# Second up-product bank, down products two units behind, and a copy moved behind the exponentials, in a four-layer attention and convolution kernel

## The chip, the cores and the metric

The kernel runs on one core of one Trainium2 chip, in one launch. The metric is the device time of that core in microseconds (us). Below, PE is TensorE, PEld its weight load, DVE VectorE, ACT ScalarE, POOL GpSimd, SP SyncE.

## The reference, cut to what matters

The input is 16 images of 128 channels by 32x32 points (1024 tokens each), float32. Four layers run one after the other; the change touches the first and the last.

```python
x = conv_attention(x)            # layer 0: group norm, qkv, softmax attention with 8 heads, projection, residual
x = x + large_kernel_conv(gn(x)) # layer 1: depthwise convolutions, gate, 1x1
t = t + landmark_attention(ln(t)); t = t + gelu_experts(ln(t))   # layer 2, 8 experts, 2 of them per token
t = t + plain_attention(ln(t))   # layer 3: q = x W + b, keys and values are the tokens themselves
t = t + silu_experts(ln(t))      # layer 3: 16 experts of width 64, 6 per token, and 2 shared ones
```

In the last line each expert computes `down(silu(gate(x)) * up(x))`, weighted by its routing score.

## The kernel before

**First stage** (`attention_phase`, about 0 to 2160 us). For each image two groups of four heads run in 64 slots. In each slot PE makes one tile of unshifted scores for a later group (L627), whose row maxima DVE takes (L454), and one tile of shifted scores (L683); ACT takes the exponentials of the two 512-column halves of that tile (L589); every fourth slot PE weighs values with them (L696). Other work of the next and the previous image is hung on single slots by `plan`. For the next image, ACT evicts the q product in slot 4 and the k product in slot 6: L565 writes `full`, L567 then copies it as bfloat16 into `pieces[:, qk, 0, :]`, and the semaphore `full_up` lets POOL cut the remaining two pieces (`split`, L399 and L401). After the second split POOL divides the previous image's sums (`divide`, L388). Both L565 and L567 stand ahead of the two exponentials of their slot on ACT.

**Last stage** (`dense_attention_and_silu`, from about 4413 us to the end; the change's title calls it the third stage). The experts are computed densely. Two experts form one unit of width 128; 8 units and one unit of shared experts make 9 (`UNITS`), and the two 512-token halves make 18 steps per image (`STEPS`). A step has three slots:

- slot 0: PE makes the gate product into the bank `ps_g` (L2214), and ACT takes its silu into one of two `act_up` buffers (L2094);
- slot 1: PE makes the up product into the single bank `ps_u` (L2217), and DVE multiplies it into `act_up` (L2021, or L2024 for the shared unit) and raises `u_read`;
- slot 2: DVE multiplies by the scores into one of two `mixed` buffers (L2028, `mixed_up`), and PE makes the down product of the step before (L2201, `down(i, n - 1)`), accumulated over 9 steps in `ps_o`.

The up product of step n waits until DVE has read the bank in step n - 1. The silu of step n waits for `mixed` of step n - 2.

Beside the steps of image i run coroutines, resumed by slot number (`due`): `choice(i + 1)`, the router (on DVE four passes over 2048 elements, L1012, L1013, L1017, L1019, and a reduction L1021), and `attention(i + 2)`: its layer norm on DVE in the first slots (L961, L966, L973), its first transposes from slot 9, its eight 128-row tiles from slot 15 on (PE L2146, L2152, L2159; DVE L1963, L1966, L1973; ACT L2056, L2059), and a second layer norm on DVE from slot 40 on. After slot 53 PE makes the last down product, DVE copies the next image's tile (`hand_over`, L2010) and the next image begins. Image 14 has only `choice` beside it, image 15 nothing. All engines run their own program in order.

The function that starts the last stage gives it PSUM banks, and buffers that earlier layers no longer use. The bank `ps_xy` was used by the layer before (L1791, L1608) and is idle in the last stage.

Of the kernel before, what the change touches and what calls it, by code (L numbers as in the profile page):

```python
# [97 lines left out]
def attention_phase(nc, sems, handles, B, io, const, const_in, band_dram, u_cols, gn2, x1_dram, split_dram, sums_dram, conv):  # L98
# [3 lines left out]
    with ExitStack() as st:  # L102
# [445 lines left out]
        def _(act):  # L548
# [9 lines left out]

            def step(work, i, nxt, prev, n, parity):
                if work[0] == "qk":  # L560
# [6 lines left out]
                    act.activation(pieces[:, qk, 0, :], full[:, qk, :], ACT.Copy)  # L567
                    act.drain().then_inc(full_up, 1)
# [14 lines left out]
            def body(kind, i):  # L583
                front, n = kind != "last", 0
                for m, works in enumerate(bodies[kind]):
                    n = run(works, kind, i, n)
                    for k in range(HALVES):
                        act.wait_ge(b_up, i * (2 * SLOTS) + 2 * m + k + 1)
                        act.activation(probs[:, m % PROBS, 512 * k:512 * k + 512], ps_b[:, k, :], ACT.Exp).then_inc(b_exp, 1)  # L589
                    if kind == "first" and m >= QUAD and m % 2 == 0 and (m - QUAD) // 2 < BANDS:  # L590
                        store_rows((m - QUAD) // 2)
# [448 lines left out]
def landmark_and_gelu_phase(nc, ctx, B, io, const, maps, gn2, x1_dram, x_dram, y_dram, score_dram, out):  # L1040
# [7 lines left out]
    with ExitStack() as st:  # L1048
# [3 lines left out]
        def sem(name):  # L1052
# [99 lines left out]
            nc, ctx, st, B, io, const, tokens, score_dram, out, flat(0, 17), (stats, mv, var, inv, tmp), (pa, pb_, *ps_h, pc), score_t, ones,  # L1152
            dict(xln=xln, xt=xt, qt=qt, probs=probs, probs_t=probs_t, xln2=tiled(kt[:, :]), xt2=wide(v[:, :, :]),
                 wg=tok_next, wu=tok, wd=tiled(xt2[:, :]), scores=up_weights, xt_now=part(0), tile_in=tiled(part(1)),
                 act_up=part(2).rearrange("p (a n) -> p a n", a=2), mixed=part(3).rearrange("p (a n) -> p a n", a=2),
# [478 lines left out]
        def _(pe):  # L1634
# [190 lines left out]
            down(B - 1, LAST)  # L1825
            run_dense()


def dense_attention_and_silu(nc, ctx, st, B, io, const, tokens, score_dram, out, small, norm, banks, score_t, ones, shared):
# [18 lines left out]
    RING = 4  # L1848
# [101 lines left out]
    def vector(dve):  # L1950
# [61 lines left out]
        def experts(i, stages):  # L2012
            for slot in range(SLOTS):
                n = slot // 3
                k, unit = divmod(n, UNITS)
                if slot % 3 == 1:
# [3 lines left out]
                    if unit < PAIRS:  # L2020
                        dve.tensor_tensor(act_up[:, n % 2, :], act_up[:, n % 2, :], ps_u[:, :], ALU.mult).then_inc(u_read, 1)  # L2021
                        dve.drain()  # L2022
                    else:
                        dve.scalar_tensor_tensor(mixed[:, n % 2, :], act_up[:, n % 2, :], 0.5, ps_u[:, :], ALU.mult, ALU.mult).then_inc(u_read, 1)  # L2024
                        dve.drain().then_inc(mixed_up, 1)
                if slot % 3 == 2 and unit < PAIRS:
                    dve.wait_ge(scores_in[unit % RING], i * (16 * HALVES * PAIRS * 2 // RING) + 32 * (k * (PAIRS // RING) + unit // RING) + 32)
                    dve.tensor_tensor(mixed[:, n % 2, :], act_up[:, n % 2, :], scores[:, unit % RING, :], ALU.mult).then_inc(mixed_up, 1)  # L2028
# [7 lines left out]
        def run(sums):  # L2036
            dve.sem_inc(u_read, 1)
# [4 lines left out]
    def scalar(act):  # L2042
# [43 lines left out]
        def experts(i, stages):  # L2086
            for slot in range(SLOTS):
                n = slot // 3
                if slot % 3 == 0:
# [5 lines left out]
                    if n == UNITS + 1:  # L2095
# [17 lines left out]
    def tensor(pe):  # L2113
# [75 lines left out]
        def down(i, n):  # L2189
# [11 lines left out]
            last = pe.matmul(ps_o[:, :], wd(unit), mixed[:, n % 2, :], start=False, stop=(unit == UNITS - 1), skip_group_check=True)  # L2201
# [3 lines left out]
        def experts(i, stages):  # L2205
            pe.wait_ge(S["xt_handed"], i + 1)
            for slot in range(SLOTS):
# [7 lines left out]
                if part == 1:  # L2215
                    pe.wait_ge(u_read, i * STEPS + n + 1)
                    pe.matmul(ps_u[:, :], wu(unit), xt_now[:, cols], start=True, stop=True).then_inc(u_ps, 1)  # L2217
                if part == 2:
                    if n:
                        down(i, n - 1)  # L2220
                for stage in stages:
                    due(stage, slot)
# [91 lines left out]
```

## Time and profile before

| | |
|---|---|
| median of 3 runs | 6012.23 us (6007.84 to 6017.8) |
| the profiled execution's own time | 6006.96 us |
| its span, first to last instruction | 6005.2 us |
| mean granted TensorE clock | 0.914 of full |
| busy: PE, DVE, ACT, POOL | 83%, 60%, 50%, 17% of the span |

A line of a group view gives: source line, engine, operation, output and inputs, count, busy time, mean duration, and the idle time of the engine just ahead of it with what ended it. In a timeline, the first number is the start, the second the duration (from first start to last end where instructions are merged, as "x8" says), and the bracket is the idle time before. A float32 matmul is shown as two passes (x2), whose modelled duration overlaps the next one's start: in the steady state one 512-column product starts 0.86 us after the one before, though its row says 1.02 us. Names of tensors are those of the memory: `n_ps_h` stands for both `ps_g` and `ps_u`, `n_ps_c` for `ps_o`, `n_down_weights` for `act_up`, `mixed` and others, `n_up_weights` for the scores.

### The profile page before, as it was taken

The numbers are of one execution on the slowest core, as the hardware profiler recorded it, in microseconds if no ns is written. First come the engines' busy times: TensorE is split into PE (matmuls) and PEld (weight loads), VectorE is DVE, ScalarE is ACT, GpSimd is POOL, SyncE is SP. The second block draws the span as 40 slices with busy tenths as digits, with TensorE's granted clock in tenths as the row PEclk, the third lists the DMA queues.
The fourth block names the chain that finished last, engine by engine and source line by source line (L and its number), as shares of the span: only waits on it lengthen the run. The fifth ranks groups of instructions, "written<-read, shape, count | busy, mean of one in ns | idle before, by whom it ended". The sixth has DMA issues, their size and how long they took to land.

```text
span 6005.2 us, 81857 instructions
## 1 busy us (share of the span) xinstructions
PE 4989.7 (83%) x25633; PEld 2720.5 (45%) x25633; DVE 3604.7 (60%) x7715; ACT 3005.7 (50%) x5436; POOL 1011.5 (17%) x1348
## 2 busy tenths in 40 slices
PE   5888888888888869577777777777888999999899
PEld 1222222222222223376676666766665555545454
DVE  6677667777767725544454444444456667676665
ACT  2555555555655534144444444444564555545453
POOL 2111122111122022022322323223210000000000
PEclk7999999999999989688888888888899999999999
DMA  2422222222222112234344334433321111111112
GB/s 78 139 80 65 75 70 91 65 86 65 65 76 85 48 38 28 62 114 131 113 121 129 116 113 132 118 114 113 100 59 48 43 49 48 44 48 45 48 45 71
DMA packets 406297, 477.10 MB, mean 79 GB/s; under 512 B 87640, under 2 KB 249648, under 8 KB 403760
## 3 DMA queue, kind: packets, MB, share of 16 engines
q1 hardware_dynamic: 372128, 424.84, 23.4%
q0 software_dynamic: 20576, 35.55, 2.1%
q10 hardware_dynamic: 13168, 11.48, 0.7%
q8 instruction: 214, 3.51, 0.2%
q14 instruction: 211, 1.73, 0.1%
HBM read 308.54 MB, written 145.57 MB: 76 GB/s over the span
## 4 chain that ended last, share of the span: by engine, by line
PE 34%; DVE 11%; another core or an unknown queue 6%; issue 4%; DVEq 2%; ACT 2%; ACTq 0%; SPq 0%; DMA 0%
PE n_ps_xy L1791 4%; PE n_ps_h L1781 4%; PE n_ps_f L2159 3%; PE n_ps_f L2152 3%; PE n_ps_c L2201 3%; PE n_ps_h L2217 3%; PE n_ps_h L2214 3%; PE n_ps_f L2146 2%; PE n_ps_f L1639 2%; PE n_ps_f L985 1%; DVE n_down_weights L2021 1%; DVE n_stats L961 1%; ACT n_hidden L1594 1%; DVEq L2022 1%
## 5 line engine op out<-in xcount | busy, mean ns | idle before, releaser
L589 ACT ACTIVATE a_probs<-ps_b 128x512 f32<-128x512 f32 x2048 | 1110.9, 594 | 805.5 <-PE ps_b L683 793.1
L454 DVE TENSOR_REDUCE a_negmax<-ps_a 128x1 f32<-128x1024 f32 x1024 | 1207.3, 1220 | 400.2 <-PE ps_a L627 390.6
L627 PE MATMUL ps_a<-a_k_stack,a_q_stack 96*128 96x512 bf16 x2048 | 640.0, 399 | 176.3 <-DVE a_negmax L454 82.9
L683 PE MATMUL ps_b<-a_q_stack,a_k_stack 99*128 99x512 bf16 x2048 | 679.8, 392 | 85.3 <-ACT a_probs L589 42.8
L1594 ACT ACTIVATE n_hidden<-n_ps_h,n_b 128x128 f32<-128x128 f32 x1472 | 420.0, 374 | 409.0 <-PE n_ps_h L1781 314.3
L696 PE MATMUL ps_o<-a_probs,a_v_ones 128*32 128x512 f32 x4096 | 561.8, 622 | 0.2 <-ACT a_probs L589 0.2
L1791 PE MATMUL n_ps_xy<-n_down_weights,n_hidden 128*128 x2944 | 436.8, 295 | 94.7 <-ACT n_xy L1608 53.9
L627 PEld LDWEIGHTS ps_a<-a_k_stack,a_q_stack 96*128 96x128 bf16 x2048 | 148.5, 99 | 732.1 <-DVE a_negmax L454 453.7
L1781 PE MATMUL n_ps_h<-n_xy,n_up_weights 128*128 128x128 f32 x2944 | 436.1, 293 | 36.6 <-issue 36.1
L1791 PEld LDWEIGHTS n_ps_xy<-n_down_weights,n_hidden 128*128 128x128 f32 x2944 | 394.9, 207 | 133.7 <-issue 130.6
L683 PEld LDWEIGHTS ps_b<-a_q_stack,a_k_stack 99*128 99x128 bf16 x2048 | 196.8, 100 | 510.1 <-ACT a_probs L589 281.3
L1781 PEld LDWEIGHTS n_ps_h<-n_xy,n_up_weights 128*128 128x128 f32 x2944 | 395.3, 206 | 60.2 <-issue 57.6
L2094 ACT ACTIVATE n_down_weights<-n_ps_h 128x512 f32<-128x512 f32 x288 | 172.4, 598 | 491.6 <-PE n_ps_h L2214 489.2
L1299 POOL DMA_INDIRECT rows_scratch<-n_xln,n_index_out x256 | 253.2, 989 | 843.8 <-DVE n_index_out L1452 766.9
L1291 POOL DMA_INDIRECT n_rows<-outs_scratch,n_index_back x256 | 255.7, 999 | 680.4 <-DMA outs_scratch<-n_xy 536.4
L2201 PE MATMUL n_ps_c<-n_down_weights,n_xt 128*128 128x512 f32 x512 | 285.1, 640 | 67.7 <-DVE n_down_weights L2028 67.6
L2217 PE MATMUL n_ps_h<-n_down_weights,n_tok 128*128 128x512 f32 x512 | 278.2, 626 | 61.8 <-DVE n_down_weights L2021 61.8
L410 POOL CAST a_shift<-a_shift 16x128 bf16<-16x128 f32 x192 | 54.2, 283 | 1335.2 <-DVEq L463 1317.8
L2159 PEld LDWEIGHTS n_ps_f<-n_xln,n_u_probs_t 128*128 128x128 f32 x2048 | 248.0, 193 | 59.9 <-issue 44.4
L2214 PE MATMUL n_ps_h<-n_down_weights,n_tok_next 128*128 128x512 f32 x512 | 273.3, 617 | 1.5 <-ACT n_down_weights L2079 1.5
L2159 PE MATMUL n_ps_f<-n_xln,n_u_probs_t 128*128 128x128 f32 x2048 | 253.0, 277 | 1.6 <-ACT n_u_probs_t L2056 1.6
L2152 PE MATMUL n_ps_f<-n_qt 128*128 128x512 f32 x512 | 242.4, 596 | 0.0
(324 smaller groups left out, 7342.3 us busy)
## 6 DMA issues: line engine op xcount, KB each, us to landing
n_up_weights<-in_L_ffn_W_dram SPq DMA_DIRECT2D x368, 256.0 KB
n_up_weights<-score_scratch SPq DMA_DIRECT2D x512, 128.0 KB
split_scratch<-a_pieces SPq DMA_DIRECT2D x180, 256.0 KB
a_q_stack<-split_scratch SPq DMA_DIRECT2D x128, 192.0 KB, 3.3
a_k_stack<-split_scratch SPq DMA_DIRECT2D x128, 192.0 KB, 3.9
rows_scratch<-n_zero SPq DMA_DIRECT2D x16, 1472.0 KB, 8.2
outs_scratch<-n_xy SPq DMA_DIRECT2D x176, 128.0 KB
n_xg<-rows_scratch SPq DMA_DIRECT2D x80, 256.0 KB
```

Of the source, the lines that this page charges most:

```text
L454: dve.tensor_reduce(negmax[:, b, t:t + 1], bank, axis=AX.X, op=ALU.max, negate=True).then_inc(ring_read, 1)
L589: act.activation(probs[:, m % PROBS, 512 * k:512 * k + 512], ps_b[:, k, :], ACT.Exp).then_inc(b_exp, 1)
L627: last = pe.matmul(bank[:, cols], q_stack[0:KS, h, 128 * t:128 * t + 128], k_stack[0:KS, h, cols], start=True, stop=True)
L683: pe.matmul(ps_b[:, k, :], k_stack[:, h, 128 * t:128 * t + 128], q_stack[:, h, 512 * k:512 * k + 512], start=True, stop=True).then_inc(b_u ...
L696: last = pe.matmul(ps_o[32 * j:32 * j + 32, 512 * k:512 * k + 512], v_ones[:, t, J * g + j, :], probs[:, (J * quad + j) % PROBS, 512 * k:5 ...
L1594: last = act.activation(hidden[:, j % 2, f, :], ps_h[j % 2][:, 128 * f:128 * f + 128], ACT.Gelu, bias=b1[:, bass.ds(e, 1), f:f + 1].rearra ...
L1781: last = pe.matmul(ps_h[j % 2][:, 128 * f:128 * f + 128], up_weights[:, j % RING, 128 * f:128 * f + 128], rows_t, start=True, stop=True)
L1791: last = pe.matmul(ps_xy[:, col:col + 128], hidden[:, j % 2, f, :], own_down[:, f, :], start=(f == 0), stop=(f == FT - 1))
L2159: last = pe.matmul(pb[:, 0:C], probs_t[:, (t - 1) % 2, m, :], xln[:, m, :], start=(m == 0), stop=(m == NT - 1))
L2201: last = pe.matmul(ps_o[:, :], wd(unit), mixed[:, n % 2, :], start=False, stop=(unit == UNITS - 1), skip_group_check=True)
L2214: pe.matmul(ps_g[:, :], wg(unit), xt_now[:, cols], start=True, stop=True).then_inc(g_ps, 1)
L2217: pe.matmul(ps_u[:, :], wu(unit), xt_now[:, cols], start=True, stop=True).then_inc(u_ps, 1)
```

## The change

In the last stage the up products alternate between two banks (`ps_h[1]` and `ps_xy`), so that the one of step n waits for DVE's reading of step n - 2. The down product of step n - 2, no longer n - 1, stands in slot 2 of step n, and two of them follow after the last slot. `mixed` has three buffers, the third in a tile of the layer before. The eviction of the first half's result on ACT moves one step later. PE waits before the stage until `ps_xy` has been emptied. In the first stage the copy L567 goes behind the two exponentials of its slot, except where the image's own prologue runs.

```diff
+            pending = []
+
+            def first_piece(qk):
+                act.activation(pieces[:, qk, 0, :], full[:, qk, :], ACT.Copy)
+                act.drain().then_inc(full_up, 1)
...
-                    act.activation(pieces[:, qk, 0, :], full[:, qk, :], ACT.Copy)
-                    act.drain().then_inc(full_up, 1)
+                    if i == nxt:
+                        first_piece(qk)
+                    else:
+                        pending.append(qk)
...
                         act.activation(probs[:, m % PROBS, 512 * k:512 * k + 512], ps_b[:, k, :], ACT.Exp).then_inc(b_exp, 1)
+                    if pending:
+                        first_piece(pending.pop())
...
-            nc, ctx, st, B, io, const, tokens, score_dram, out, flat(0, 17), (stats, mv, var, inv, tmp), (pa, pb_, *ps_h, pc), score_t, ones,
+            nc, ctx, st, B, io, const, tokens, score_dram, out, flat(0, 17), (stats, mv, var, inv, tmp), (pa, pb_, ps_h[0], (ps_h[1], ps_xy), pc), score_t, ones,
...
+            pe.wait_ge(moved, B * PAIRS + 2)
             run_dense()
...
-                        dve.tensor_tensor(act_up[:, n % 2, :], act_up[:, n % 2, :], ps_u[:, :], ALU.mult).then_inc(u_read, 1)
+                        dve.tensor_tensor(act_up[:, n % 2, :], act_up[:, n % 2, :], ps_u[n % 2][:, :], ALU.mult).then_inc(u_read, 1)
...
-                    dve.tensor_tensor(mixed[:, n % 2, :], act_up[:, n % 2, :], scores[:, unit % RING, :], ALU.mult).then_inc(mixed_up, 1)
+                    dve.tensor_tensor(mixed[(i * STEPS + n) % 3], act_up[:, n % 2, :], scores[:, unit % RING, :], ALU.mult).then_inc(mixed_up, 1)
...
-            dve.sem_inc(u_read, 1)
...
-                    if n == UNITS + 1:
+                    if n == UNITS + 2:
                         store_half(i, 0)
...
-                    pe.wait_ge(u_read, i * STEPS + n + 1)
-                    pe.matmul(ps_u[:, :], wu(unit), xt_now[:, cols], start=True, stop=True).then_inc(u_ps, 1)
+                    if started(i) or n >= 2:
+                        pe.wait_ge(u_read, i * STEPS + n - 1)
+                    pe.matmul(ps_u[n % 2][:, :], wu(unit), xt_now[:, cols], start=True, stop=True).then_inc(u_ps, 1)
                 if part == 2:
-                    if n:
-                        down(i, n - 1)
+                    if n >= 2:
+                        down(i, n - 2)
                 for stage in stages:
                     due(stage, slot)
+            down(i, STEPS - 2)
             down(i, STEPS - 1)
```

## Rows read from the trace of the kernel before

**Rows 1.** The page: span, and each engine's busy time.

```profile
span 6005.2 us, 81857 instructions
PE 4989.7 (83%) x25633; PEld 2720.5 (45%) x25633; DVE 3604.7 (60%) x7715; ACT 3005.7 (50%) x5436; POOL 1011.5 (17%) x1348
```

**Rows 2.** Window, images 0 to 14: length, busy PE, PEld, DVE, ACT, POOL, clock.

```profile
4413.00:5950.00 1537.00, 1390.48 (x5702) 791.04 (x5702) 1027.08 (x2383) 780.98 (x979) 15.22 (x16) 0.97 0.15 49
```

**Rows 3.** Waits of PE from 4413 us on: total us, times, longest.

```profile
PE n_ps_c L2201 <- DVE n_down_weights L2028: 67.6, 49, 3.9
PE n_ps_h L2217 <- DVE n_down_weights L2021: 61.8, 28, 12.0
```

**Rows 4.** Windows of one image of the last stage, in three stretches.

```profile
5143.50:5162.60 19.10, 15.10 (x33) 5.91 (x32) 12.30 (x46) 3.45 (x5) 0.00 (x0) 0.91 0.18 55
5162.60:5192.40 29.80, 25.70 (x85) 12.83 (x83) 25.83 (x58) 12.64 (x17) 0.00 (x0) 0.94 0.17 51
5192.40:5247.50 55.10, 54.38 (x277) 35.50 (x278) 31.92 (x61) 38.40 (x47) 0.00 (x0) 1.00 0.13 41
```

**Rows 5.** Timeline of the end of one image, PE and DVE, from step 13 on.

```profile
5144.70 1.65 DVE L961 BATCH_NORM_STATS2 n_stats<-maps 128x6 f32<-128x128 f32 x8
...
5151.08 0.69 DVE L2021 TENSOR_TENSOR n_down_weights<-n_down_weights,n_ps_h 128x512 f32<-128x512 f32 x1
...
5151.82 1.12 PE L2217 MATMUL n_ps_h<-n_down_weights,n_tok 128*128 128x512 f32 x2 [2.84 <-DVE n_down_weights L2021]
...
5155.13 1.92 PE L2214 MATMUL n_ps_h<-n_down_weights,n_tok_next 128*128 128x512 f32 x2
...
5158.28 0.69 DVE L2021 TENSOR_TENSOR n_down_weights<-n_down_weights,n_ps_h 128x512 f32<-128x512 f32 x1 [2.02 <-PE n_ps_h L2217]
...
5160.86 0.69 DVE L2024 SCALAR_TENSOR_TENSOR n_down_weights<-n_down_weights,n_ps_h 128x512 f32<-128x512 f32 x1 [1.10 <-PE n_ps_h L2217]
...
5162.61 1.02 PE L2214 MATMUL n_ps_h<-n_down_weights,n_tok_next 128*128 128x512 f32 x2
```

**Rows 6.** Timeline of the start of the next image, up to its first attention tiles.

```profile
5165.47 0.69 DVE L2021 TENSOR_TENSOR n_down_weights<-n_down_weights,n_ps_h 128x512 f32<-128x512 f32 x1 [0.42 <-PE n_ps_h L2217]
...
5175.66 0.69 DVE L2021 TENSOR_TENSOR n_down_weights<-n_down_weights,n_ps_h 128x512 f32<-128x512 f32 x1 [0.66 <-ACT n_down_weights L2094]
...
5186.26 0.69 DVE L2021 TENSOR_TENSOR n_down_weights<-n_down_weights,n_ps_h 128x512 f32<-128x512 f32 x1 [0.77 <-PE n_ps_h L2217]
...
5189.89 1.22 DVE L1966 TENSOR_REDUCE e_negmax<-n_ps_f 128x1 f32<-128x1024 f32 x1
...
5192.41 1.09 PE L2146 MATMUL n_ps_f<-c_ident,n_yt_probs 128*128 128x128 f32 x8 [0.25 <-ACT n_yt_probs L2059]
```

**Rows 7.** Waits of DVE from 4413 us on.

```profile
DVE n_down_weights L2021 <- PE n_ps_h L2217: 79.8, 83, 3.8
...
DVE n_down_weights L2024 <- PE n_ps_h L2217: 19.1, 18, 1.1
```

**Rows 8.** Waits of PE from 5895 to 5950 us: image 14, with only the router beside it.

```profile
PE n_ps_c L2201 <- DVE n_down_weights L2028: 5.9, 3, 3.9
```

**Rows 9.** Timeline of image 15: two gate products, one step apart.

```profile
5990.35 1.02 PE L2214 MATMUL n_ps_h<-n_down_weights,n_tok_next 128*128 128x512 f32 x2
...
5992.93 1.02 PE L2214 MATMUL n_ps_h<-n_down_weights,n_tok_next 128*128 128x512 f32 x2
```

**Rows 10.** Timeline of the first stage around one k product: ACT, PE, POOL.

```profile
1018.75 1.11 ACT L565 ACTIVATE a_full<-ps_a,a_kbias 128x1024 f32<-128x1024 f32 x1 [1.96 <-PE ps_a L653]
...
1019.95 1.06 ACT L567 ACTIVATE a_pieces<-a_full 128x1024 bf16<-128x1024 f32 x1
...
1021.11 3.31 ACT L589 ACTIVATE a_probs<-ps_b 128x512 f32<-128x512 f32 x6
...
1021.76 0.88 PE L683 MATMUL ps_b<-a_q_stack,a_k_stack 99*128 99x512 bf16 x2 [0.75 <-ACT a_probs L589]
...
1031.72 2.47 POOL L388 TENSOR_TENSOR a_o_sums<-a_o_sums,a_recips 128x256 f32<-128x256 f32 x3 [1.21 <-DMA a_recips<-sums_scratch]
```

More of the change, by code:

```diff
@@ L1151, in landmark_and_gelu_phase @@
         dense = dense_attention_and_silu(
-            nc, ctx, st, B, io, const, tokens, score_dram, out, flat(0, 17), (stats, mv, var, inv, tmp), (pa, pb_, *ps_h, pc), score_t, ones,
+            nc, ctx, st, B, io, const, tokens, score_dram, out, flat(0, 17), (stats, mv, var, inv, tmp), (pa, pb_, ps_h[0], (ps_h[1], ps_xy), pc), score_t, ones,
             dict(xln=xln, xt=xt, qt=qt, probs=probs, probs_t=probs_t, xln2=tiled(kt[:, :]), xt2=wide(v[:, :, :]),
                  wg=tok_next, wu=tok, wd=tiled(xt2[:, :]), scores=up_weights, xt_now=part(0), tile_in=tiled(part(1)),
-                 act_up=part(2).rearrange("p (a n) -> p a n", a=2), mixed=part(3).rearrange("p (a n) -> p a n", a=2),
+                 act_up=part(2).rearrange("p (a n) -> p a n", a=2), mixed=[part(3)[:, 0:512], part(3)[:, 512:1024], xg[:, 0, :, :].rearrange("p t c -> p (t c)")],
                  result=hidden[:, :, :, :].rearrange("p a f n -> p a (f n)")))
@@ L2020, in experts @@
                     if unit < PAIRS:
-                        dve.tensor_tensor(act_up[:, n % 2, :], act_up[:, n % 2, :], ps_u[:, :], ALU.mult).then_inc(u_read, 1)
+                        dve.tensor_tensor(act_up[:, n % 2, :], act_up[:, n % 2, :], ps_u[n % 2][:, :], ALU.mult).then_inc(u_read, 1)
                         dve.drain()
                     else:
-                        dve.scalar_tensor_tensor(mixed[:, n % 2, :], act_up[:, n % 2, :], 0.5, ps_u[:, :], ALU.mult, ALU.mult).then_inc(u_read, 1)
+                        dve.scalar_tensor_tensor(mixed[(i * STEPS + n) % 3], act_up[:, n % 2, :], 0.5, ps_u[n % 2][:, :], ALU.mult, ALU.mult).then_inc(u_read, 1)
                         dve.drain().then_inc(mixed_up, 1)
@@ L2200, in down @@
             pe.wait_ge(mixed_up, i * STEPS + n + 1)
-            last = pe.matmul(ps_o[:, :], wd(unit), mixed[:, n % 2, :], start=False, stop=(unit == UNITS - 1), skip_group_check=True)
+            last = pe.matmul(ps_o[:, :], wd(unit), mixed[(i * STEPS + n) % 3], start=False, stop=(unit == UNITS - 1), skip_group_check=True)
             if unit == UNITS - 1:
```

## The prediction

> **What bounds the kernel now.** I read the page first, then windows by stage, then the waits of the last stage, then one image of it in the timeline. The page has PE busy for 83% of the span and DVE for 60% [rows 1], but these are means over stages. In the last stage, images 0 to 14, PE is busy 1390 of 1537 us [rows 2], so about 147 us are idle there. Most of that idle time is two waits for DVE: 67.6 us before down products and 61.8 us before up products, 129.4 us together [rows 3]. These are the two waits that the change moves by a unit. The temptation is to subtract them. Whether they can be had depends on what DVE is doing meanwhile.
>
> One image shows it. Its period is 104.0 us (19.10 + 29.80 + 55.10) and falls into three stretches [rows 4]. In the third, the attention tiles, PE is busy 54.38 of 55.10 us at full clock: PE is the bound and nothing is to be had. In the second, the router, DVE is busy 25.83 of 29.80 us. In the first, the layer norm at the image's end, PE is busy 15.10 and DVE 12.30 of 19.10 us, the clock is at 0.91, and DVE waits for PE as well as PE for DVE. So outside the tiles the two engines share a chain. Once the up product has a second bank, PE waits less, but DVE's own work stays in line and becomes the bound. What the change can give back is then the time in which DVE itself stood waiting for an up product, and not the time in which PE stood waiting for DVE.
>
> **The change part by part.**
>
> *End of an image (steps 13 to 17).* DVE starts the layer norm at 5144.70 and reaches the multiplication of step 14 only at 5151.08; PE's up product of step 14 + 1 waits for exactly that and starts at 5151.82 after 2.84 us of idling [rows 5]. From there PE is a unit late: DVE waits 2.02 us for the up product of step 16 and 1.10 us for that of step 17 [rows 5]. In the new order the up product of step 16 needs only the reading of step 14, which is over at 5151.08 + 0.69 = 5151.77. It can start near 5151.8, and DVE wants it at 5158.28 - 2.02 = 5156.26: ready. The up product of step 17 needs the reading of step 15. The silu of each step still waits for the second multiplication of two steps before, which here precedes by more than the 0.60 us of a silu, so ACT does not take over. DVE's chain then runs without these waits and closes 2.02 + 1.10 = 3.12 us earlier. PE can follow: from 5144.70 to the next image's first gate product it has 14 products at 0.86 us (a third of the 2.58 us between the gate products of image 15 [rows 9]), 12.0 us, and 5144.7 + 12.0 = 5156.7 is ahead of 5162.61 - 3.12 = 5159.49. Both trailing down products fit: the second-last one runs while DVE does L2024, the last one follows it as today. What may be lost is clock. In this stretch the clock is granted at 0.91, so 0.09 x 19.10 = 1.7 us of PE work is missing [rows 4]; a gate product at the lower of its two levels (1.2 instead of 2.4 GHz) takes 1.92 instead of 1.02 us [rows 5]. PE still idles some 2.8 us there afterwards (5159.49 - 5156.7), so a half-clock stretch probably stays. PE has that slack only until the last products, which it can make late by part of the 1.7 us. Bounds 3.12 and 3.12 - 1.7 = 1.4 us; I take 2.7, since most of the slack lies ahead of the last three products.
>
> *Start of an image (steps 0 to 5).* DVE waits 0.42 us for the very first up product, which no second bank makes earlier, 0.66 us for a silu that stands on ACT behind the router's exponential and its table, and 0.77 us for the up product of step 4 [rows 6]. The first two stay. The third goes, as PE is a unit ahead by then. PE's other idle time there only changes place: it will run ahead, make the early products of the attention, and then stand before the transposes of tile 1, which wait for the exponential that follows DVE's maximum L1966 (5189.89) [rows 6]. That maximum is behind the router passes on DVE, and DVE is in line for it. So the start gives 0.77 us at best, 0 at worst if PE's half clock just there eats it; I take 0.75.
>
> *The tiles.* PE's order has one down product shifted by a unit and the same number of them. Nothing.
>
> Together 2.7 + 0.75 = 3.45 us per image, for images 0 to 13: 48.3 us. A check from the other side: over the stage DVE waits 79.8 + 19.1 = 98.9 us for up products [rows 7], in 101 cases, about a third to a half of it in places that stay (first product of an image, and image 15, where DVE waits each step because PE is the bound). 14 x (3.12 + 0.77) = 54.5 us is the part that I call recoverable.
>
> *Image 14.* Only the router is beside it, PE waits 5.9 us for DVE before down products [rows 8], DVE being the bound for some five steps, and being free afterwards. A unit of run-ahead is two products, 1.7 us, and the 0.77 us kind of wait goes too. Bounds 0 and 5.9, I take 3 (half). *Image 15* runs at PE's pace, 2.58 us a step [rows 9]: nothing, the end perhaps 0.2 us.
>
> *Waits added and moves.* PE's wait for `ps_xy` to be emptied stands where PE already waits for the hand-over on ACT, whose program has the emptying ahead of it: nothing. The later eviction of the first half has behind it on PE the first down product of the second half, which moved by a step too: nothing. SP's loads of scores wait for `mixed_up`, which DVE raises as before.
>
> *First stage.* L567 takes 1.06 us and stands ahead of six exponentials in a row (3.31 us); PE waits 0.75 us for the first of them [rows 10]. Behind them it lets two exponentials begin 1.2 us earlier, but the next two then wait for it. ACT's work up to the end of the six is the same, 1.11 + 1.06 + 3.31 us, and PE's shifted scores, at one exponential each, meet the same finish one slot later. So the stall moves by a slot. What is gained is at most that 0.75 us in 15 images, 11 us, and at least nothing. Queued behind the later `full_up` is POOL: its cuts end about 1.15 us later, and then `divide`, which today waits 1.21 us for a DMA [rows 10], so it just fits. If it did not, the loss would be the 1.06 us at most, 16 us in 15 images, and only if the projection, 20 slots later, were waiting for it. I take 0, nearest to the rows.
>
> **The sum.** 48.3 + 3 + 0.2 + 0 = 51.5 us. From the profiled execution's own 6006.96 us (1.8 us around the span of 6005.2) that gives 5955.5 us. The median of the runs is 6012.23, 5.3 us higher, and it is what the result will be compared with: 6012.2 - 51.5 = 5961 us.
>
> The Trainium skill speaks against the change in its page "TensorE: Matmul & The Clock Gate", section "HAM oscillation — how this bites in real kernels": for a kernel whose loop had already been put in the better order, "Adding PSUM double-buffering gave no further gain". Read as a rule for this kernel it makes the time 6012 us, and rival 3 is its case; the trace so far has DVE idle before up products, which speaks for a gain.
>
> **The rivals.**
>
> 1. *All of PE's waits go.* If DVE had free time to catch up, 129.4 us [rows 3] would go: 6012 - 129 = 5883 us. For it: the size of the waits. Against it: DVE busy 25.83 of 29.80 us in the router stretch. Chance 0.04.
> 2. *Less, for the clock.* The half-clock stretch falls on the last products of each image and the start gives nothing: 1.4 us x 14 = 20 us, image 14 gives 1: 5991 us. For it: the clock at 0.91 and 0.94 in the two stretches. Against: PE's slack. Chance of 5976 to 6000 in all: 0.17.
> 3. *No gain.* DVE's waits reappear elsewhere, because the silu, still with two `act_up` buffers, comes to be what DVE waits for (0.66 us once per image today [rows 6]); each up-product wait is replaced by one for L2094. 6012 us. Chance 0.07.
> 4. *Slower, by the clock.* PE now stands before the transposes of tile 1, directly ahead of the stretch in which it is the bound. If the idle time there brings the low level into the tiles, each such stretch costs 1.7 us (as priced above) with nothing to hide it. The gain of 3.45 us per image is used up by two of them, and from three per image on the kernel is slower: 14 x (5.1 - 3.45) = 23 us, 6035 us. For it: the clock does fall after idle time. Against: the tiles now run at 1.00 although PE idled just ahead of them, and one stretch at most has its cause there. Chance 0.04.
>
> **How the numbers follow.** My forecast, 5945 to 5976 us, has 0.68, likeliest 5961. Its own range comes from the bounds: all of 54.5 + 5.9 us plus some of the first stage's 11 gives 5945; 2.4 us per image and little else 5976. For 8 in 10 the range reaches into rival 2: 5942 to 5990. Changes of under 0.2% (12 us) can't be told from none by such a measurement. Faster by more, below 6000: 0.68 + 0.04 + 0.17 = 0.89, of which I move 0.01 to the others for what I have not seen: 0.88. Same 0.07, slower 0.05.
>
> **What would show it.** In the changed profile: the waits of L2021 and L2024 for L2217 down by some 50 us, those of PE for L2028 and L2021 down by less than half of their 129 us or turned into waits of L2146 for the exponential; an image's period near 100.5 us instead of 104.0; DVE without gaps from the layer norm to the next image's hand-over; the tiles' stretch unchanged at 55 us and full clock; the first stage's length unchanged within a few us, with one wait of L683 moved by a slot. It would be wrong if the period stayed at 104 (rival 3), if the clock in the tiles fell under 1.00 (rival 4), or if DVE's passes turned out to be delayed by something other than their order.

## The result, and the profile after

The changed kernel takes 5938.8 us (median of 4 runs, 5937.2 to 5940.5), the kernel before in the same comparison 6012.6 us: ratio 0.988, 95% interval 0.986 to 0.989, 73.7 us less. The forecast was 5961 us and its range ended at 5942, so the time lies just below the range. The sign was right; the size was short by three tenths. Of all the runs below one, of `first_only`, took 6367 us at a granted clock of 0.80 and is left out of its median.

The page of the changed kernel, against [rows 1]; the span is 66.5 us shorter, where the medians differ by 73.7: the profile before lies 5.3 us under its median and the one after 1.7 us over it:

```profile
span 5938.7 us, 81856 instructions
PE 4964.3 (84%) x25633; PEld 2725.1 (46%) x25633; DVE 3599.3 (61%) x7715; ACT 3001.1 (51%) x5436; POOL 1007.4 (17%) x1348
```

No engine has less to do. PE's idle time falls from 1015.5 to 974.4 us, by 41.1, and the same 25633 matmuls are busy 25.4 us less, at a mean granted clock of 0.917 for 0.914. To see where, I cut both timelines at two places: the start of the last exponential of the first stage, and the first hand-over of the last stage on ACT.

| stretch | before, us | after, us | difference | forecast |
|---|---|---|---|---|
| first stage | 2148.4 | 2122.6 | -25.8 | 0 |
| middle stages | 2265.2 | 2274.4 | +9.2 | 0 |
| last stage, to the end | 1591.6 | 1541.7 | -49.9 | -51.5 |

So the part on which nearly all of the prediction's working was spent came out within 2 us, and the part that got one paragraph and a zero did not.

**The last stage.** Windows of the changed kernel: images 0 to 14, against [rows 2], and then one image in the same three stretches as [rows 4] (length, busy PE, PEld, DVE, ACT, POOL, granted clock):

```profile
4396.50:5884.00 1487.50, 1374.60 (x5701) 796.19 (x5701) 1023.59 (x2383) 781.29 (x979) 15.51 (x16) 0.97 0.16 50
5103.86:5120.98 17.12, 15.42 (x35) 6.43 (x34) 12.21 (x46) 3.44 (x5) 0.00 (x0) 0.90 0.19 62
5120.98:5149.93 28.95, 24.58 (x84) 13.18 (x82) 25.74 (x58) 12.64 (x17) 0.00 (x0) 0.94 0.19 54
5149.93:5205.63 55.70, 54.98 (x282) 35.97 (x283) 31.91 (x61) 38.48 (x47) 0.00 (x0) 1.00 0.13 40
```

The image's end is 1.98 us shorter, the router's stretch 0.85 us. The tiles' stretch is a little longer because PE makes some of its products there (282 matmuls for 277), at full clock. Over images 1 to 13 the mean period (hand-over to hand-over) went from 104.3 to 101.0 us.

Waits of PE in the last stage of the changed kernel (total us, times, longest), against [rows 3]:

```profile
PE n_ps_h L2224 <- ACT n_down_weights L2104: 59.9, 15, 14.0
PE n_ps_c L2211 <- DVE n_xg L2039: 12.1, 16, 1.4
PE n_ps_h L2228 <- DVE n_down_weights L2032: 11.7, 14, 2.2
PE n_ps_f L2156 <- ACT n_yt_probs L2069: 11.4, 14, 2.7
...
PE n_ps_c L2211 <- DVE n_down_weights L2039: 4.1, 14, 1.1
```

and waits of DVE there, against [rows 7]:

```profile
DVE n_down_weights L2032 <- PE n_ps_h L2228: 24.6, 32, 2.6
...
DVE n_down_weights L2032 <- PE n_ps_xy L2228: 18.7, 25, 2.0
...
DVE n_xg L2035 <- PE n_ps_xy L2228: 3.5, 4, 1.1
...
DVE n_xg L2035 <- PE n_ps_h L2228: 1.1, 1, 1.1
```

PE's 129.4 us of waits for DVE shrank to 12.1 + 11.7 + 4.1 = 27.9 us, but 59.9 us now stand before gate products for the silu, and the waits before the transposes grew from 3.2 to 11.4 us. DVE's waits for up products fell from 98.9 to 47.9 us, that is by 51.0 us: the time that the stage gained. The second number is the one to forecast from.

The end of the same image in the changed kernel's timeline (start, duration, idle time before), against [rows 5]:

```profile
5115.19 0.69 DVE L2032 TENSOR_TENSOR n_down_weights<-n_down_weights,n_ps_xy 128x512 f32<-128x512 f32 x1 [0.19 <-issue]
5115.98 0.69 DVE L2039 TENSOR_TENSOR n_down_weights<-n_down_weights,n_up_weights 128x512 f32<-128x512 f32 x1
5116.59 0.68 DVE L2032 TENSOR_TENSOR n_down_weights<-n_down_weights,n_ps_h 128x512 f32<-128x512 f32 x1
...
5118.68 0.69 DVE L2035 SCALAR_TENSOR_TENSOR n_xg<-n_down_weights,n_ps_xy 128x512 f32<-128x512 f32 x1 [0.63 <-PE n_ps_xy L2228]
```

The 2.02 us wait is gone, the 1.10 us one is 0.63: DVE's multiplications follow each other as soon as the layer norm lets them.

**The first stage.** One image of the kernel before, from the eviction of q to that of k:

```profile
492.26 1.11 ACT L565 ACTIVATE a_full<-ps_a,a_qbias_d 128x1024 f32<-128x1024 f32 x1 [2.69 <-PE ps_a L653]
...
493.46 1.06 ACT L567 ACTIVATE a_pieces<-a_full 128x1024 bf16<-128x1024 f32 x1
...
495.27 0.88 PE L683 MATMUL ps_b<-a_q_stack,a_k_stack 99*128 99x512 bf16 x2 [0.71 <-ACT a_probs L589]
...
499.16 1.11 ACT L565 ACTIVATE a_full<-ps_a,a_kbias 128x1024 f32<-128x1024 f32 x1 [1.96 <-PE ps_a L653]
```

and the same place in the changed kernel:

```profile
486.53 1.11 ACT L571 ACTIVATE a_full<-ps_a,a_qbias_d 128x1024 f32<-128x1024 f32 x1 [3.09 <-PE ps_a L663]
...
487.73 1.09 ACT L597 ACTIVATE a_probs<-ps_b 128x512 f32<-128x512 f32 x2
...
488.67 0.60 PE L693 MATMUL ps_b<-a_q_stack,a_k_stack 99*128 99x512 bf16 x2
488.70 1.06 ACT L562 ACTIVATE a_pieces<-a_full 128x1024 bf16<-128x1024 f32 x1
...
492.27 1.11 ACT L571 ACTIVATE a_full<-ps_a,a_kbias 128x1024 f32<-128x1024 f32 x1 [0.81 <-PE ps_a L663]
```

Before, q's piece copy holds back two exponentials and PE waits 0.71 us for them. After, the copy runs behind the exponentials, PE does not wait at L693, and the k product is done 1.16 us earlier (5.74 us from q to k instead of 6.90). The edit saves time at q's copy. [Rows 10] show k's copy, and the image that I had read for q was the one evicted at 1011.86 us, in the kernel before:

```profile
1011.55 1.06 PE L627 MATMUL ps_a<-a_k_stack,a_q_stack 96*128 96x512 bf16 x2
```

Right behind q's product PE still ran at the lower clock there (1.06 us for a pair of products that take 0.60 us elsewhere), and the copy hid behind the slower PE: no wait before L683, and 6.89 us from q to k all the same.

### The profile page after: what moved, and what is told of

Its sections match the earlier page's. It is cut to its first block, busy times and chain, and to the rows that moved or that the text cites. A ratio compares the mean times of both kernels' runs of the same rounds, so it can differ in the third digit from the quotient of the medians.

```text
span 5938.7 us, 81856 instructions
## 1 busy us (share of the span) xinstructions
PE 4964.3 (84%) x25633; PEld 2725.1 (46%) x25633; DVE 3599.3 (61%) x7715; ACT 3001.1 (51%) x5436; POOL 1007.4 (17%) x1348
## 4 chain that ended last, share of the span: by engine, by line
PE 32%; DVE 12%; another core or an unknown queue 5%; issue 5%; DVEq 3%; ACT 2%; ACTq 0%; SPq 0%; DMA 0%
PE n_ps_xy L1801 4%; PE n_ps_h L1791 4%; PE n_ps_f L2169 3%; PE n_ps_f L2162 3%; PE n_ps_c L2211 2%; PE n_ps_h L2224 2%; PE n_ps_f L2156 2%; PE n_ps_f L1649 2%; PE n_ps_xy L2228 1%; DVEq L2033 1%; PE n_ps_h L2228 1%; DVE n_down_weights L2032 1%; PE n_ps_f L995 1%; DVE n_stats L971 1%
## 5 line engine op out<-in xcount | busy, mean ns | idle before, releaser
L693 PE MATMUL ps_b<-a_q_stack,a_k_stack 99*128 99x512 bf16 x2048 | 673.0, 391 | 66.7 <-ACT a_probs L597 30.9
L693 PEld LDWEIGHTS ps_b<-a_q_stack,a_k_stack 99*128 99x128 bf16 x2048 | 196.2, 100 | 486.0 <-ACT a_probs L597 247.1
L2224 PE MATMUL n_ps_h<-n_down_weights,n_tok_next 128*128 128x512 f32 x512 | 274.0, 618 | 61.4 <-ACT n_down_weights L2104 59.9
L2169 PEld LDWEIGHTS n_ps_f<-n_xln,n_u_probs_t 128*128 128x128 f32 x2048 | 248.0, 193 | 59.9 <-issue 44.7
L1977 DVE TENSOR_REDUCE e_negmax<-n_ps_f 128x1 f32<-128x1024 f32 x128 | 156.6, 1223 | 124.1 <-PE n_ps_f L2162 124.1
L2069 ACT ACTIVATE n_yt_probs<-n_ps_f,e_negmax 128x1024 f32<-128x1024 f32 x128 | 142.5, 1114 | 120.9 <-DVE e_negmax L1977 120.4
```

What stands on the lines that cost most here:

```text
L693: pe.matmul(ps_b[:, k, :], k_stack[:, h, 128 * t:128 * t + 128], q_stack[:, h, 512 * k:512 * k + 512], start=True, stop=True).then_inc(b_u ...
L2169: last = pe.matmul(pb[:, 0:C], probs_t[:, (t - 1) % 2, m, :], xln[:, m, :], start=(m == 0), stop=(m == NT - 1))
L2224: pe.matmul(ps_g[:, :], wg(unit), xt_now[:, cols], start=True, stop=True).then_inc(g_ps, 1)
```

## The experiments

Each ratio is against the kernel before on the same chip; its median was 6041.0 us for the first four runs, 6038.9 us for the next four, 6004.1 us for the last two.

**1. Each half of the change alone.** `first_only` has only the first stage's edit, `last_only` only the last stage's (two banks, down products two behind, three buffers).

> The first stage's edit alone (both copies behind the exponentials). In the changed kernel's trace the first stage ends 25.8 us earlier and the middle stages are 7 us longer. Theory A, the copy itself is worth it: the kernel is 14 to 26 us faster than before, 5987 to 5998 us, because at full clock the q product's copy held up PE's next shifted scores by about 1.2 us per image. Theory B, nothing of it is the copy's doing and the stage is shorter by the luck of the clock: 6008 to 6016 us, with a first stage as long as before within 5 us.

Measured: 6018.9 us, ratio 0.9959 [0.9944, 0.9973], 22.1 us faster.

> The last stage's edit alone. Theory A (DVE's own waits for up products are what comes back): period 100.8 instead of 104.1 us per image, 48 to 52 us in the stage, 5960 to 5965 us. Rival: the two edits help each other through the clock, and alone it gives less than 40 us, above 5972 us.

Measured: 5988.0 us, ratio 0.9914 [0.9891, 0.9937], 53.0 us faster. The two add up to 75.1 us, the change gave 73.7 us. So within the intervals (9 and 14 us to either side) the halves are independent, and the first stage's gain is real: about 22 us where the prediction had 0.

The profiles of all the runs say the same. In the four whose first stage is that of before (`before`, `last_only`, `banks_only`, `downs_only`) its last exponential starts at 2148.4, 2143.7, 2142.0 and 2147.0 us; in the five with both copies moved (`first_only`, the changed kernel, `after_again`, `router_later`, `third_silu`) at 2129.6, 2122.6, 2135.5, 2125.9 and 2125.1 us. The two groups do not overlap, and their means differ by 17.5 us.

**2. The first stage's edit, q's copy and k's copy apart.** In `q_only` k's copy stays where it was, in `k_only` q's:

```
+                    if i == nxt or qk == 1:      # q_only;  k_only: qk == 0
+                        first_piece(qk)
+                    else:
+                        pending.append(qk)
```

> The first stage's edit for the q product (slot 4) alone. Theory A: the q copy carries nearly all, since slot 4 also has the copy of v on ACT behind it; 90 to 100 percent of the gain of the first stage's edit, q-to-k distance 5.74 instead of 6.90 us at full clock. Rival: the k copy carries it, and this one stays within 5 us of before.

Measured: 6033.7 us, ratio 0.9982 [0.9967, 0.9997].

> The first stage's edit for the k product (slot 6) alone. Theory A: three slots of exponentials follow the k copy without a gap, so the stall of 0.75 us only moves: 0 to 3 us faster. Rival: it gives the 0.75 us in each of 15 images, 11 us.

Measured: 6037.9 us, ratio 0.9995 [0.9982, 1.0007]. The expectation for `k_only` holds, that for `q_only` (nearly the whole gain) does not: by the medians neither alone comes near 22 us (7.3 and 3.1 us), though the interval of `q_only` reaches 20. To see why, I read the same intervals of images 1 to 13 in each profile. The 42 us from v to the attention column agree to 0.02 us in every image, and the rest, from attention to the next q, varies by up to 2 us from image to image, whatever the kernel; what differs between kernels is this (sums over 13 images, us):

```
kernel        q to k   k to v   attention around the normalization
before          89.7    106.6    504.2
q_only          81.4    110.8    503.3
k_only          89.6    102.4    496.9
first_only      80.7    102.4    493.7
changed         80.4    102.3    494.6
q_fed           80.9    103.8    493.6   (experiment 3)
changed, 2nd    83.5    102.4    503.3   (experiment 5)
```

The q edit saves about 8 us before the k product, and `q_only` then loses 4 us before the v product. Windows of `q_only`, from q to k and from k to v, of one image:

```profile
362.80:368.54 5.74, 5.74 (x30) 1.69 (x29) 2.45 (x2) 4.74 (x7) 2.14 (x3) 1.00 0.01 0
368.54:377.94 9.40, 8.15 (x40) 3.26 (x39) 5.31 (x6) 5.42 (x8) 8.06 (x10) 0.82 0.29 64
```

of the kernel before:

```profile
492.26:499.16 6.90, 6.09 (x30) 1.69 (x29) 2.45 (x2) 4.75 (x8) 3.99 (x5) 1.00 0.02 5
499.16:507.14 7.98, 6.70 (x39) 3.02 (x38) 5.26 (x6) 5.42 (x8) 6.78 (x9) 1.00 0.14 38
```

and of the changed kernel:

```profile
486.53:492.27 5.74, 5.74 (x30) 1.68 (x29) 2.45 (x2) 4.74 (x7) 2.13 (x3) 1.00 0.03 6
492.27:500.14 7.87, 6.72 (x39) 3.02 (x38) 5.26 (x5) 5.30 (x8) 6.69 (x8) 1.00 0.12 24
```

In `q_only` PE is busy all of 5.74 us, a gain of 1.16, and in the next stretch the clock is granted at 0.82, part of it at the lower of the two levels (1.2 instead of 2.4 GHz): 9.40 us instead of 7.98. That happens in 5 of 13 images (the expectation of experiment 3 says 6), all 5 among the 6 whose q to k took 5.74 or 5.75 us. In the four profiles with the first stage of before it happens in 2, 1, 0 and 2 of 13. With k's copy moved too it never does: 7.87 or 7.88 us each time, in all five profiles.

**3. Is it the clock?** `q_fed` is `q_only` with one repetition: in the slot right behind k's eviction, in which PE waits 0.75 us for an exponential [rows 10], the score products are made twice, so that PE is busy instead. The repetition changes no result.

```
-                        last = pe.matmul(bank[:, cols], q_stack[...], k_stack[...], start=True, stop=True)
+                        for _ in range(fed):          # 2 in slot 7, else 1
+                            last = pe.matmul(bank[:, cols], q_stack[...], k_stack[...], start=True, stop=True)
```

> The kernel before with the q copy moved alone, and in slot 7 each score product is made twice, so that PE has 0.9 us more work just where it would stand and wait for the first exponential (same result; only PE works more). In the run with the q copy alone, the 1.16 us gained before the k product is followed in 6 of 13 images by a stretch at half clock between the k product and the eviction of v (9.4 instead of 8.0 us). Theory C, that stretch follows from PE's idling there: with PE fed, the distance is near 8.1 to 8.5 us in nearly all images and never 9.4. Rival: the clock falls for idle time further back, and 9.4 us or more stays in some six images.

Measured: 6022.7 us, ratio 0.9967 [0.9952, 0.9982]; k to v is 7.98 us in all 13 images. With more work for PE the kernel is not slower than `q_only`. By the two ratios it is 9 us faster, but they come from two chips and their intervals overlap, so the times alone do not show a gain. The profiles do: the 9.40 us stretches are gone (7.0 us less from k to v), the attention column is 9.7 us less, and the first stage ends at 2128.0 instead of 2145.8 us. So what `q_only` lost before the v product went to the clock.

The third column of the table, attention, is of the same kind. The changed kernel has no instruction less there. It is the 37 to 41 us around the first normalization, and its short stretch ends at an eviction on ACT. Windows of one image of the kernel before, the two stretches around the first normalization:

```profile
678.87:683.85 4.98, 4.10 (x24) 0.96 (x24) 3.40 (x21) 3.26 (x7) 1.68 (x5) 1.00 0.01 2
683.85:718.18 34.33, 29.68 (x139) 7.67 (x139) 26.07 (x23) 19.72 (x36) 0.00 (x0) 0.90 0.29 93
```

and of the changed kernel:

```profile
289.14:295.66 6.52, 5.71 (x25) 1.19 (x26) 4.86 (x22) 3.26 (x6) 1.67 (x5) 0.74 0.11 31
295.66:326.25 30.59, 26.86 (x139) 7.13 (x137) 24.54 (x22) 19.71 (x36) 0.00 (x0) 1.00 0.31 97
```

One half-clock stretch comes either way. Falling in the short stretch it costs 1.5 us, falling in the long one 3 to 5. The cheap case was met by 3 of 13 images before and by 9 of 13 after, and that makes the 10 us of the third column.

How much of it is the edit's doing can be read from the other profiles. With the first stage of before, 18 of 52 images meet the cheap case (3, 6, 4 and 5 of 13) and the column is 500.4 us on the mean (497.5 to 504.2); with both copies moved 37 of 65 do (9, 9, 3, 8 and 8), and it is 496.4 us (493.6 to 503.3). So 10 us is a lucky pair of profiles and some 4 us the mean. And in the five profiles with both copies moved the case hangs on the same image's q to k: of the 37 images in which it took at most 6.4 us, 35 met the cheap case, of the 28 in which it took 6.59 us or more, 2. So the edit has a part in it: an image that has run from q to k at full clock nearly always has this half-clock stretch where it is cheap. In `q_only`, where the 9.40 us stretch comes in between, it is 2 of 7.

**4. The last stage's edit, its two parts apart.** `banks_only` has the two banks and three buffers with the down product one unit behind; `downs_only` has one bank, and the down product two behind with three buffers:

```
 banks_only:
+                    if started(i) or n >= 2:
+                        pe.wait_ge(u_read, i * STEPS + n - 1)
 ...
                     if n:
                         down(i, n - 1)
 downs_only:
+                    if started(i) or n >= 1:
+                        pe.wait_ge(u_read, i * STEPS + n)
 ...
+                    if n >= 2:
+                        down(i, n - 2)
```

> Last stage only: the second up bank alone, down products one unit behind as before, first stage as before. Worked through the end of an image: the up product of step 16 comes in time (2.0 us of DVE's wait go), that of step 17 still stands behind a down product that waits for DVE (1.1 us stay), and in the head the 0.77 us stays. Theory A: 14 x 2.0 = 28 us, 20 to 35 us faster than before. Rival: the second bank is all that matters, and it gives the full 50 us.

Measured: 6050.5 us, ratio 1.0014 [1.0000, 1.0027]: no gain, and a last stage 12 us longer in its profile.

> Last stage only: down products two units behind with three mixed buffers, but one up bank as before, first stage as before. Theory A: PE no longer stands before a down product, but each up product still waits for the reading of the step before: about 1.8 us of the end and 0.77 us of the head, 14 x 2.5 = 35 us, 25 to 40 us faster. Rival: without the bank nothing is gained, within 10 us of before.

Measured: 6031.0 us, ratio 0.9987 [0.9973, 1.0001]. Theory A missed in both: by the medians `banks_only` has none of the 53 us and `downs_only` 7.9, less than a quarter (its interval reaches 16), which is its rival, "within 10 us of before". PE's waits in `banks_only`, where L2201 is the down product and L2029 the second multiplication:

```profile
PE n_ps_c L2201 <- DVE n_xg L2029: 74.0, 30, 4.7
PE n_ps_c L2201 <- DVE n_down_weights L2029: 59.1, 29, 14.2
```

and in `downs_only`, where L2218 is the up product and L2022 the first multiplication:

```profile
PE n_ps_h L2218 <- DVE n_down_weights L2022: 105.8, 37, 15.1
PE n_ps_f L2146 <- ACT n_yt_probs L2059: 26.2, 14, 2.2
```

Each removes one of the two waits and keeps the total. `banks_only` has 133.1 us for 129.4 before; `downs_only` has 105.8 and 26.2 before the transposes, 132.0 us, for 129.4 and 3.2 before. DVE's waits for up products are again what goes with the time: 112.5 us in `banks_only` and 78.0 in `downs_only` for 98.9 before, while the stage takes 1604.0 and 1580.9 us for 1591.6. `banks_only` shows how, at the image's end (DVE, then PE):

```profile
5181.87 0.68 DVE L2029 TENSOR_TENSOR n_xg<-n_down_weights,n_up_weights 128x512 f32<-128x512 f32 x1
...
5188.21 0.69 DVE L2022 TENSOR_TENSOR n_down_weights<-n_down_weights,n_ps_h 128x512 f32<-128x512 f32 x1 [2.97 <-PE n_ps_h L2218]
```

```profile
5182.61 2.08 PE L2201 MATMUL n_ps_c<-n_xg,n_xt 128*128 128x512 f32 x2 [3.83 <-DVE n_xg L2029]
5184.48 1.91 PE L2214 MATMUL n_ps_h<-n_down_weights,n_tok_next 128*128 128x512 f32 x2
5186.19 1.91 PE L2218 MATMUL n_ps_h<-n_down_weights,n_tok 128*128 128x512 f32 x2
```

PE's order is gate, up, down. The up product has its bank free, but it is queued behind a down product that still waits for the second multiplication of the unit before; it begins at 5186.19, at half clock after 3.83 us of idling, and DVE waits 2.97 us for it. At the image's end the second multiplication of a unit and the first one of the next run back to back on DVE (in the changed kernel at 5115.98 and 5116.59), so the two waits of PE end within one DVE instruction of each other: lifting one leaves the other. Only together do they give PE a unit of slack. By stretch (my cut of the timelines at the layer norm's first instruction and at the hand-over, both on DVE, means of images 1 to 13, us):

```
kernel        hand-over to layer norm   layer norm to hand-over    sum
before                86.91                     17.41             104.3
banks_only            86.62                     18.68             105.3
downs_only            85.95                     17.63             103.6
last_only             86.32                     14.90             101.2
changed               86.10                     14.89             101.0
```

The start's gain (0.8 us) comes with the down products alone; the end's gain (2.5 us) comes only with both. That a wait of the one kind takes the other's place is shown here by `banks_only`'s timeline; for `downs_only` it is read from the totals.

The Trainium skill's page "TensorE: Matmul & The Clock Gate", section "HAM oscillation — how this bites in real kernels", says of its kernel that PSUM double-buffering "gave no further gain". For the second bank by itself `banks_only` agrees (ratio 1.0014), for the bank with the deeper order `last_only` does not (0.9914).

**5. What bounds the last stage now?** PE stands 59.9 us for the silu. First try, `router_later`: if DVE's router passes are what is late, their place should matter.

```
-            yield from spread(7, gate_choose_steps(dve, gate, E, K, 1e-9, tie[:, :]), 3)
+            yield from spread(10, gate_choose_steps(dve, gate, E, K, 1e-9, tie[:, :]), 3)
```

> The changed kernel, with the router's passes from slot 10 on instead of 7 (three slots apart as before), in the last stage: one pass of 2.29 us less ahead of the attention tiles, one more within them. If DVE's chain now bounds the head (theory A), each of 14 images is up to 2.3 us shorter, 15 to 32 us faster than the changed kernel, near 0.983 of before. Rival: the tiles, where PE is the bound, pay for the pass by a later row maximum, and the time stays within 6 us of the changed kernel's.

Measured: 5970.6 us, ratio 0.9880 [0.9857, 0.9902], that of the changed kernel; period 101.4 us. The silu's waits are what they were: one of 3.3 to 3.8 us in each of images 1 to 13, the same to 0.02 us as in the changed kernel, one of 0.75 us, and the long one of 14.0 us in image 0, which only has another name in this view. New are waits of the router's own product:

```profile
PE n_ps_h L2224 <- ACT n_down_weights L2104: 45.8, 14, 3.8
PE n_ps_f L2189 <- DVE maps L1984: 20.0, 14, 1.7
PE n_ps_h L2224 <- issue: 14.0, 1, 14.0
```

Second try, `third_silu`: a third buffer for the silu's output, beside the changed kernel itself on the same chip (`after_again`).

```
-                    if n >= 2:
-                        act.wait_ge(mixed_up, i * STEPS + n - 1)
-                    act.activation(act_up[:, n % 2, :], ps_g[:, :], ACT.Silu).then_inc(silu_up, 1)
+                    if n >= 3:
+                        act.wait_ge(mixed_up, i * STEPS + n - 2)
+                    act.activation(act_up[n % 3], ps_g[:, :], ACT.Silu).then_inc(silu_up, 1)
```

> The changed kernel with a third buffer for the silu's output, so that the silu of a step waits for the second multiplication of three steps before instead of two. In the changed kernel PE stands 59.9 us in the last stage before gate products for the silu, and the silu stands for the second multiplication on DVE. Theory A (the silu's wait only hides DVE's lateness: DVE is in line outside the attention tiles): the waits of PE move to the down products or the up products, the period stays within 0.3 us of 101.0 us, the time is that of the changed kernel within 5 us. Theory B (the buffer is a limit of its own, because the silu itself, 0.6 us, comes after DVE's multiplication at each stalled step): some 0.6 us at about three stalled steps per image, 1.8 us a period, 25 us less than the changed kernel, and PE's waits for the silu nearly gone.

> The changed kernel unchanged, on the same chip as the run with a third silu buffer, so that the two can be compared. Expected ratio 0.988 as measured before; in the profile the interval from the eviction of q to that of k in the first stage 5.74 us in most images and from k to v always 7.87 us.

Measured: `third_silu` 5938.3 us, ratio 0.9885 [0.9864, 0.9906]; `after_again` 5947.4 us, 0.9892 [0.9872, 0.9912]: no difference that can be told. In `third_silu`:

```profile
PE n_ps_h L2224 <- ACT n_xg L2104: 59.2, 15, 13.4
PE n_ps_f L2156 <- ACT n_yt_probs L2069: 21.1, 14, 2.7
```

PE still waits 59.2 us for the silu with a third buffer, and the period is 100.95 us. So the time is theory A's, but the waits did not move to the other products as it said. The buffer is no limit.

What makes the silu late stands in the changed kernel's timeline, at the start of the image after the one above (lines of three engines):

```profile
5127.08 1.02 PE L2224 MATMUL n_ps_h<-n_down_weights,n_tok_next 128*128 128x512 f32 x2
...
5131.46 0.29 DVE L1011 TENSOR_TENSOR n_small<-n_small,e_gate_top 128x128 f32<-128x128 f32 x1
...
5131.79 0.31 ACT L2077 ACTIVATE n_small<-n_small 128x128 f32<-128x128 f32 x1 [5.26 <-DVE n_small L1011]
5132.12 1.28 ACT L2104 ACT_TABLE_LOAD   x1
...
5133.41 0.60 ACT L2104 ACTIVATE n_down_weights<-n_ps_h 128x512 f32<-128x512 f32 x1
5134.04 0.69 DVE L2032 TENSOR_TENSOR n_down_weights<-n_down_weights,n_ps_h 128x512 f32<-128x512 f32 x1 [0.66 <-ACT n_down_weights L2104]
5134.06 1.28 PE L2224 MATMUL n_ps_h<-n_down_weights,n_tok_next 128*128 128x512 f32 x2 [3.35 <-ACT n_down_weights L2104]
```

The gate product of step 2 is done at 5128.10. Its silu stands on ACT behind the router's exponential (L2077), which waits 5.26 us for DVE's last step before it (L1011), and behind the table that is loaded after it (1.28 us). Over the stage this exponential waits so in 15 images, 14 times for L1011 (72.6 us in all) and 13.6 us in image 0. The second multiplication and the buffer had nothing to do with it, and `router_later` moved only passes that come after this exponential. PE's next gate product waits 3.35 us for the silu, but DVE only 0.66 us, in this kernel as before [rows 6]. DVE sets the pace, so moving the exponential would give at most some 0.66 us in 14 images, 9 us. This is an estimate from these waits, and no run tests it.

`after_again` missed its expectation in the first stage: q to k is 5.74 or 5.75 us in only 5 of images 1 to 13. So it is in the first profile of the same kernel, but there four more take at most 6.4 us, here none. The run tells how much of that stage's gain was luck. Its last exponential starts at 2135.5 us, 12.9 us later than in the first profile: the last column of the table in experiment 2 is back at 503.3. And its middle stages take 2269.0 us, 5.4 us less than the same kernel's first profile.

## Why the prediction was right and wrong

**First stage, forecast 0: the step that failed.** "So the stall moves by a slot", and the bounds 0 to 11 us with 0 taken, were argued from k's copy in one image [rows 10]. The edit touches two copies. For k's I was nearly right: in the changed kernel PE's wait of 0.75 us became one of 0.36 us for a row maximum and one of 0.28 us for an exponential, and the interval from k to v changes by 0.11 us at full clock. For q's copy the step was wrong: only two exponentials stand behind it, the copy then fits behind them without a stall, and 1.16 us is gained in each image in which PE runs from q to k at full clock, 6 to 9 us over images 1 to 13 (first column of experiment 2's table). To this come 4.3 us before the v product in these two profiles (0.11 us in each image, and two half-clock stretches that no longer occur), and half-clock stretches that fall in a cheaper place, 10 us in the best pair of profiles and 4 us on the mean. One profile has the stage 25.8 us shorter, the second 12.9 us, the means of four and five profiles differ by 17.5 us, and the medians of `first_only` give 22.1 us. Even the upper bound of 11 us left out the clock. Had the term been 22, the sum would have been 5939 us; that this is the measured median is partly luck, as the profiles vary by more than it is off.

**Middle stages, forecast 0.** +9.2 us in the one profile. The change edits nothing in them, and they vary between executions by as much: four profiles on one chip, alike in these stages, have 2288.7 to 2298.8 us (`q_only`, `first_only`, `last_only`, `k_only`), and four on another 2295.0 to 2308.7 us (`banks_only`, `downs_only`, `router_later`, `q_fed`). So the 9.2 us can't be told from zero.

**End of an image, forecast 2.7 of 3.12 us.** 2.5 us on the mean. Right, and the reason too: DVE's waits for up products went, and the clock at 0.90 kept a part.

**Start of an image, forecast 0.75 us.** 0.8 us. Right in size. But it comes from the down products two behind, since `banks_only` has 0.3 us of it, where the prediction had PE "a unit ahead by then". PE's idle time does change place, but mostly not to the transposes of tile 1, as the prediction said: it stands before a gate product, behind the router's exponential on ACT (experiment 5).

**Image 0 and image 14, forecast 3.45 and 3 us.** From hand-over to hand-over on DVE image 0 gave 4.6 us (118.5 to 113.9) and image 14 1.5 us (61.6 to 60.1); the two terms together are right. With 13 x 3.3 us the stage gives 49 us of the 49.9.

**The tiles and the added waits, forecast 0.** Full clock in the tiles, and none of the added waits shows among PE's waits of the stage.

**The check from DVE's side** (54.5 us recoverable of 98.9) was the best number of all: 51.0 us went, 3.5 less.

**The rivals.** All of PE's waits going: 101.5 of 129.4 us went by name, and 68.1 us came back under other names (59.9 before gate products, 8.2 more before the transposes). No gain: refuted for the change, but it is what each of its parts does alone, and I had not seen that when I set the expectations of experiment 4. Slower by the clock: the tiles stayed at 1.00. Less, for the clock: not in the last stage, while in the first stage the clock moved both ways by about as much as the edit itself (8 us before the k product).

No version here beats the changed kernel by more than can be told.

## What to carry to other kernels

Ask of a gain how long the engine that sets the pace stood waiting, and not how long the others waited for it. When an engine has two waits that end within one instruction of each other, lift both or neither. When an edit touches an instruction that runs in several places, read each place, in more than one image, and look at the granted clock of the image that you read: a half-clock stretch hides the very stall that the edit removes.

## What the runs showed of the hardware

- A gain on PE can be taken back by its clock: in `q_only`, of the 6 images that gained the full 1.16 us from q to k, 5 have a following stretch granted at 0.82 (in the one read) that takes 9.4 instead of 7.98 us.
- Work that nobody needs need not cost time: with score products made twice in one slot the 9.4 us stretches vanish and the first stage's profile is 17.8 us shorter. The ratios, 0.9967 for 0.9982, overlap in their intervals.
- Where a half-clock stretch falls decides what it costs: 37.1 us (6.52 + 30.59) when it lies in the short stretch, 39.3 us (4.98 + 34.33) in the long one. With both copies moved, it falls in the short one in 35 of 37 images that ran from q to k in at most 6.4 us, and in 2 of 28 others. Two profiles of one kernel differ by 13 us in the first stage, and 8.7 us of this are in these two stretches.
- An engine that waits long need not be the one to help: PE's 3.35 us wait for a silu behind the router's exponential costs DVE, which sets the pace, 0.66 us.
